# A LayerNorm, attention and mixture-of-experts block on one core: normalising on GpSimd, turning by DMA, and the output projection by half batches

## The reference

```python
xn = _layernorm(x)
q = (xn @ Wq + bq).reshape(B, T, 8, 128)
k, v = split(xn @ Wkv + bkv)
q, k = q + pe, k + pe
probs = softmax(causal(q @ k.T / sqrt(128)))
s = (probs @ v) @ Wo                      # heads side by side
logits = xn @ router_w + router_b         # the two largest of 8 are kept
y = sum_e gating[e] * (relu(xn @ w1[e] + b1[e]) @ w2[e] + b2[e])
x = x + s * silu(y)
```

## Time and profile before

| | us |
|---|---|
| median of 3 runs | 1088.56 (1087.25 to 1088.9) |
| the profiled execution | 1086.89 |
| its span, first to last instruction | 1085.0 |
| TensorE's granted clock, mean | 0.999 of full |

### The profile page before, as it was taken

One profiled execution on the slowest core, in us unless ns is written; L12 is line 12 of the kernel. 1 busy time (PEld: TensorE's weight loads), 2 busy tenths in 40 slices (PEclk: granted clock), 3 DMA queues, 4 the chain that ended last, 5 costly groups with the idle time before them and its releaser, 6 DMA issues.

```text
span 1085.0 us, 25159 instructions
## 1 busy us (share of the span) xinstructions
PE 995.2 (92%) x8734; PEld 783.7 (72%) x8734; DVE 859.1 (79%) x1543; ACT 644.6 (59%) x1360; POOL 324.9 (30%) x339
## 2 busy tenths in 40 slices
PE   1647999999999999998889889999999999999997
PEld 1536888888888898965656667767677677777776
DVE  6885777666766555569999999998999999999971
ACT  3812333233333333348888888878888888888860
POOL 0005999899994200020011102121112111112111
PEclk9999999999999999999999999999999999999999
DMA  8548776766665312137897888998999879898992
GB/s 281 178 192 182 154 186 172 173 175 178 178 171 157 89 50 55 37 102 147 165 162 141 158 159 177 164 149 153 171 185 178 148 147 170 160 173 160 175 183 90
DMA packets 402810, 168.80 MB, mean 156 GB/s; under 512 B 345562, under 2 KB 393252, under 8 KB 402052
## 3 DMA queue, kind: packets, MB, share of 16 engines
q1 hardware_dynamic: 345632, 127.04, 56.1%
q10 hardware_dynamic: 50580, 22.45, 8.6%
q0 software_dynamic: 6480, 17.70, 6.6%
HBM read 51.66 MB, written 30.67 MB: 76 GB/s over the span
## 4 chain that ended last, share of the span: by engine, by line
PE 35%; DVE 13%; DMA 3%; ACT 3%; issue 2%; SPq 0%; ACTq 0%; DVEq 0%
PE b_psS L1144 10%; PE b_psO L1167 10%; PE b_psJ L1183 5%; PE b_psJ L1101 4%; DVE b_ph L1383 4%; DVE b_nmax L1347 4%; DMA b_pT<-b_ph 3%; PE b_psS L1194 2%; PE b_psS L1101 1%; PE b_psO L1169 1%; DVE b_outs L1389 1%; ACT b_pr L1252 1%; ACT b_ph L1282 1%; DVE b_psJ L1356 1%; PE b_psS L1147 1%
## 5 line engine op out<-in xcount | busy, mean ns | idle before, releaser
L847 PE MATMUL psU<-bxT,w_p 128*128 128x256 f16 (+1 forms) x1920 | 287.9, 263 | 13.3 <-DVE w_p L273 10.4
L922 ACT ACTIVATE h<-psU,bias 128x256 f32<-128x256 f32 (+1 forms) x320 | 124.7, 447 | 284.9 <-PE psU L847 192.8
L856 PE MATMUL psY<-w_p,hp 128*128 x1704 | 272.4, 273 | 1.8 <-DVE hp L944 1.3
L1144 PE MATMUL b_psS<-b_kp,b_Q 128*128 128x512 f16 (+3 forms) x1152 | 218.4, 326 | 0.1
L847 PEld LDWEIGHTS psU<-bxT,w_p 128*128 x1920 | 189.1, 98 | 33.8 <-issue 15.1
L1252 ACT ACTIVATE b_pr<-b_psS,b_nmax 128x1024 f32<-128x1024 f32 (+7 forms) x256 | 186.7, 734 | 42.4 <-DVE b_nmax L1347 22.8
L1167 PE MATMUL b_psO<-b_pT,b_vp 128*128 128x256 f16 x1536 | 188.6, 272 | 18.1 <-issue 8.4
L1383 DVE SCALAR_TENSOR_TENSOR b_ph<-b_pr,b_rrec,b_ph 128x1024 f16<-128x1024 f32 (+7 forms) x256 | 199.1, 809 | 0.0
L1282 ACT ACTIVATE b_ph<-b_pr,b_rrec 128x1024 f16<-128x1024 f32 (+7 forms) x256 | 187.0, 768 | 15.9 <-DVE b_rrec L1376 15.6
L942 DVE CAST hp<-h 128x512 f16<-128x512 f32 (+1 forms) x160 | 88.5, 553 | 134.0 <-ACT h L922 127.1
L1347 DVE TENSOR_REDUCE b_nmax<-b_psS 128x1 f32<-128x1024 f32 (+7 forms) x256 | 182.7, 745 | 9.2 <-PE b_psS L1147 7.3
(11 more groups left out here) (181 smaller groups left out, 1029.4 us busy)
## 6 DMA issues: line engine op xcount, KB each, us to landing
wstage<-in_L_ffn_w SPq DMA_DIRECT2D x48, 256.0 KB
expert_rows<-rowx SPq DMA_DIRECT2D x67, 128.0 KB
expert_outputs<-y ACTq DMA_DIRECT2D x31, 256.0 KB
a_x_all<-in_L_attn_x SPq DMA_DIRECT2D x8, 512.0 KB, 9.8
a_w_raw<-in_L_ffn_w SPq DMA_DIRECT2D x4, 1024.0 KB, 6.5
xn_split<-a_xp SPq DMA_DIRECT2D x4, 1024.0 KB, 4.9
xn_turned<-a_xT SPq DMA_DIRECT2D x3, 1024.0 KB, 12.8
b_x_row<-in_L_attn_x SPq DMA_DIRECT2D x24, 128.0 KB, 2.6
```

The source lines that it names most:

```text
L847: mm = eng.matmul(psU[w % U][:, g % 2, 0:tiles * P].rearrange("p (t r) -> p t r", t=tiles), weight(n, a * W1 + c * H + g * P, P), bxT[n % ...
L856: mm = eng.matmul(psY[n % 2][:, t, :], hp[n % 2][:, a, g, t * P:(t + 1) * P], weight(n, 2 * W1 + (2 * g + b) * D, D), start=(g == 0 and k ...
L922: a = eng.activation(h32[w % 4][:, g, 0:rows], psU[w % U][:, g, 0:rows], ACT.Relu, bias=bias[:, ds(e * HT + 2 * q + g, 1)], scale=1.0 / WS)
L1144: mm = eng.matmul(dst, Q[n % 3][:, a, u * P:(u + 1) * P], kb[:, c, lo:lo + w], start=(kk == 0), stop=(kk == 2 and not last))
```

## The change

**Routing.** The first eight pairs are normalised by GpSimd instead of DVE, which goes on to the second half's statistics at once. The pairs 0, 2, 4, ... 12 are turned by DMAs that SP issues ahead of its four row stores, and no longer by PE and ACT; PE, ACT and DVE keep the other nine. ACT's order is written anew, so that the second root comes after six high halves.

**Attention.** The output projection goes by half batches: from n = 5 on, at i = 4, `o_pair` makes two tiles through four heads, again 24 matmuls, but into all of `psJ`. Where it is the first half of the batch's heads, ACT copies the bank out (`o_part`, 128x512); where the second, DVE adds the bank to that copy (`o_sum`, 128x512), and GpSimd multiplies by the gates and adds x (`weighted`, `added`, both 128x512). There are 28 of these calls instead of 24, so `rows_out` has only heads 28 to 31 left. The gates come from n = 4 on, one a head, and three a head in heads 30 and 31, in order of the tiles. The first half of the last batch is weighted and added to x ahead of the closing. DVE's second `o_low` of a head moves behind the maxima of step 0. There is one `outs`, x of the last batch has its own place and is loaded in head 8, and ACT waits for the last expert output to be stored ahead of head 0.

The diff, cut to its core:

```diff
-    OUT_DVE = (TWOS - 3, TWOS - 1)
+    BY_DMA = tuple(range(0, TWOS - 2, 2))
+    BY_PE = tuple(p for p in range(TWOS) if p not in BY_DMA)
...
-        for p in range(TWOS):
-            turn(p)
-            if p == 3:
+        eng.wait_ge(s_rl, 1)
+        for e in range(len(BY_PE)):
+            turn(e)
+            if e == 1:
                 eng.wait_ge(s_br, 80)
-            if p >= 2:
-                logits(p - 2)
+            if 1 <= e <= 7:
+                logits(BY_PE[e - 1])
+            if e >= 2 and e - 2 < len(BY_DMA) - 1:
+                logits(BY_DMA[e - 2])
+        logits(BY_DMA[-1])
...
+        behind = {7: 1, 8: 3, 9: 5, 11: 7, 13: 9, 15: 11}
+        root(0)
+        for p in range(6):
+            high(p)
+        root(1)
+        for p in range(6, TWOS):
+            high(p)
+            if p in behind:
+                out(behind[p])
+        out(TWOS - 3)
+        out(TWOS - 1)
...
-        for p in range(4):
-            normal(p)
-            after(p)
         for g in (5, 6, 7):
             stats(g)
-            normal(g - 1)
-            after(g - 1)
         variance(NT, slice(HALF, NT))
-        normal(7)
-        after(7)
+        eng.wait_ge(s_rh, 1)
+        eng.scalar_tensor_tensor(rw_p[:, 1], rw_s[:, :, :], WS, rw_p[:, 0], ALU.mult, ALU.subtract).then_inc(s_rl, 1)
+        for p in range(4):
+            low(p)
         rstd(2, slice(HALF, NT))
         for p in range(8, TWOS):
             normal(p)
-            after(p)
-        for p in range(TWOS, TWOS + 3):
-            after(p)
+            low(p - 4)
+        for p in range(TWOS - 4, TWOS):
+            low(p)
+        out(TWOS - 2)
...
+        eng.wait_ge(s_rs, 1)
+        for p in range(TWOS // 2):
+            for t in (2 * p, 2 * p + 1):
+                a = eng.tensor_scalar(x_all[:, t, :], x_all[:, t, :], mv[:, t, 0:1], rs[:, 0, t:t + 1], ALU.subtract, ALU.mult)
+            a.then_inc(s_xp, 1)
...
+        for d, p in enumerate(BY_DMA):
+            low_done(eng, p)
+            if d >= 4:
+                eng.wait_ge(s_dt[d % 4], 16 * (d // 4))
+            eng.dma_start_transpose(turned(p).rearrange("p t h n -> p (t h) n"),
+                                    xp[:, 2 * p:2 * p + 2].rearrange("p t h d -> p (t h d)")).then_inc(s_dt[d % 4], 16)
...
-    seq = list(range(TILES, NT)) + list(range(TILES))
-    turn_of = {c: s for s, c in enumerate(seq)}
+    PART, MORE = HEADS // 2, TILES // 2
+    gates = [(5 * n + 1, n - PART) for n in range(PART, NH - 2)]
+    gates += [(5 * n + x, NT - 6 + 3 * (n - NH + 2) + x) for n in (NH - 2, NH - 1) for x in range(3)]
+    gate_at = dict(gates)
...
+        outs = sb("outs", [P, 2, HEADS, T], F16)
+        fin = sb("x_last", [P, QT, D], F32)
...
-            def o_tile(c):
+            def o_pair(r):
+                m, p = r // 4, r % 4
+                eng.wait_ge(al_, 2 * PART * (m + 1))
+                if r:
+                    bank_free(eng, r - 1)
+                h0 = PART * (m % 2)
+                for x in range(2):
+                    t = 2 * p + x
+                    for h in range(h0, h0 + PART):
+                        for kk, (a, e) in enumerate(PASSES):
+                            mm = eng.matmul(psJ[:, x * D:(x + 1) * D], outs[:, a, h, t * P:(t + 1) * P], wo_p[:, e, h, :],
+                                            start=(x == 0 and h == h0 and kk == 0), stop=(x == 1 and h == h0 + PART - 1 and kk == 2))
...
-                        if i == 0 and n >= HEADS + 2:
-                            eng.wait_ge(ot_, n - HEADS - 1)
+                        if i == 0 and n >= PART + 2:
+                            bank_free(eng, n - PART - 2)
                         project(*jobs.order[q], job_bank[jobs.bank[q]]).then_inc(jm_, 1)
-                    if i == 4 and n > HEADS:
+                    if i == 4 and n > PART:
                         eng.wait_ge(jl_, jobs.issued(k + 1))
-                        o_tile(n - HEADS - 1)
+                        o_pair(n - PART - 1)
...
-            rows_out(0, 0, HEADS - 2)
-            o_tile(TILES - 1)
+            rows_out(0, PART, HEADS - 2)
+            o_pair(NH - PART - 1)
...
-            rows_out(3, 0, HEADS - 1)
+            rows_out(3, PART, HEADS - 1)
...
-            rows_out(2, 0, HEADS - 1)
+            rows_out(2, PART, HEADS - 1)
...
-            rows_out(1, 0, HEADS - 1)
+            rows_out(1, PART, HEADS - 1)
...
+            def o_part(g):
+                eng.wait_ge(om_, 4 * (2 * (g // 4)) + g % 4 + 1)
+                if g >= 4:
+                    eng.wait_ge(oa_, g - 3)
+                eng.activation(part[g % 4][:, :, :].rearrange("p t d -> p (t d)"), psJ[:, :], ACT.Copy, scale=0.5 / WS).then_inc(oe_, 1)
...
+            for i, o in enumerate(v["y_o"]):
+                eng.wait_ge(o, 16 * len(range(i, NBLK, 3)))
...
+                if i == 0 and n >= PART + 2 and not two_of(n - PART - 2)[0]:
+                    o_part(two_of(n - PART - 2)[1])
...
-                if k < LAST and n:
-                    if i == 1:
-                        weigh(seq[n - 1])
-                    if i == 3:
-                        tanh(seq[n - 1])
-            weigh(TILES - 1)
-            tanh(TILES - 1)
+                if k in gate_at:
+                    weigh(gate_at[k])
+                if k - 2 in gate_at:
+                    tanh(gate_at[k - 2])
+            o_part(two_of(NH - PART - 1)[1])
...
-                if 2 <= c < TILES:
-                    eng.wait_ge(oa_, c - 1)
+                if 8 <= c < TILES:
+                    eng.wait_ge(oa_, c // 2 - 3)
...
+            def o_sum(g):
+                whole = part[g % 4][:, :, :].rearrange("p t d -> p (t d)")
+                eng.wait_ge(oe_, g + 1)
+                eng.wait_ge(om_, 4 * (2 * (g // 4) + 1) + g % 4 + 1)
+                eng.scalar_tensor_tensor(whole, psJ[:, :], 0.5 / WS, whole, ALU.mult, ALU.add).then_inc(ot_, 1)
...
-                if i == 0 and n >= HEADS + 2:
-                    o_gated(n - HEADS - 2)
+                if i == 0 and n >= PART + 2 and two_of(n - PART - 2)[0]:
+                    o_sum(two_of(n - PART - 2)[1])
...
-                if 6 <= k <= LAST and (k - 1) % 5 in (2, 4):
-                    o_low((k - 1) // 5 - 1, (k - 1) % 5 // 4)
+                if 6 <= k <= LAST and i == 3:
+                    o_low(n - 1, 0)
                 if k < LAST:
                     maxima(k)
+                if 6 <= k <= LAST and i == 0:
+                    o_low(n - 2, 1)
-                if k < LAST and n:
-                    if i == 2:
-                        whole_f(seq[n - 1])
-                    if i == 4:
-                        gated(seq[n - 1])
+                if k - 1 in gate_at:
+                    whole_f(gate_at[k - 1])
+                if k - 3 in gate_at:
+                    gated(gate_at[k - 3])
...
             o_low(NH - 1, 0)
+            eng.wait_ge(fe_, 4)
             closing(0)
...
+            def weighted(g):
+                eng.wait_ge(G_, max(turn_of[2 * g], turn_of[2 * g + 1]) + 1)
+                eng.tensor_tensor(flat(part[g % 4][:, :, :]), flat(part[g % 4][:, :, :]), flat(G_of(g)), ALU.mult).then_inc(og_, 1)
+                eng.wait_ge(og_, g + 1)
+            def added(g):
+                eng.wait_ge(ot_, g + 1)
+                weighted(g)
+                eng.wait_ge(xq[g % 3], 16 * (g // 3 + 1))
+                eng.tensor_tensor(flat(xr[g % 3][:, :, :]), flat(part[g % 4][:, :, :]), flat(xr[g % 3][:, :, :]), ALU.add).then_inc(oa_, 1)
...
+                if i == 1 and n >= PART + 2:
+                    second, g = two_of(n - PART - 2)
+                    if second:
+                        added(g)
+                    elif g >= MORE:
+                        added_last(g)
+                if k + 3 in gate_at:
+                    fetch(gate_at[k + 3])
+            added_last(MORE + 3)
...
-            eng.wait_ge(sc_, LAST)
-            eng.dma_start(fin[:, :, :], xf[:, TILES:, :]).then_inc(xf_, 16)
+                if i == 1 and n == HEADS:
+                    eng.dma_start(fin[:, :, :], xf[:, TILES:, :]).then_inc(xf_, 16)
```

172 lines of the change are left out of this document (75 added, 97 removed).

## The result

The changed kernel takes 1093.57 us in the median of 8 runs (1090.57 to 1102.04), the kernel before 1087.9 us in 8 runs beside them (1085.9 to 1095.13). The ratio is 1.0063, with a 95% interval from 1.0044 to 1.0081: 0.6% slower, where I had forecast 1% faster. The profiled execution took 1092.46 us, 5.6 us above that of before.

What follows compares the result with a forecast made beforehand. Bounds: routing's chain up to the logits, DVE in the first heads, PE from head 5 on. -4.4 - 3.5 + 4.5 + 1.5 + 2.3 - 10.4 = -10.0 us gave 1076.9, 1078.6 as median; range 1070 to 1087 us.

Steps and rivals of the forecast that it cites:

- Routing, -4.4 forecast: Routing up to the logits: last low half 7.2 us earlier, 2.8 given back behind it; between -6.5 and 0.
- signs of being wrong: Last head: PE waits for turned probabilities; routing: GpSimd's normalising over 0.7 us; heads 10 to 29 growing longer.
- ScalarE's saved copies: Routing: seven copies at 1.00 us that ACT no longer makes, said to count for nothing more.
- Heads 1 to 4, -3.5 forecast: DVE-bound first heads lose gates and a wait: 1.06 us a head in three, 0.3 in head 4; -4 to -1.5.
- the wait: Heads 1 to 3: DVE's 0.33 us wait goes with `o_low` behind the maxima.
- Heads 5 to 10, +4.5 forecast: `o_pair` brings PE 24 more matmuls a head: +3.6 in heads 5 to 7, +0.9 in 8 to 10; +3 to +6.
- later heads, +1.5 forecast: Heads after 10: same PE work, small costs from `o_part` and GpSimd beside DVE's low halves; between 0 and 10 us.
- Rival (b): GpSimd and DVE hinder each other behind the twelve `o_sum`: 1.7 us a head, 20 us, 3.3 in routing; 1099 us, chance 0.07.
- the cover that I named for `o_part`: Later heads: 1.46 us of score matmuls and the maxima behind them hide `o_part`; any excess would be paid 16 times.
- Heads 30 and 31 and the end, -8.1 forecast: Extra gates and gathers cost heads 30 and 31 +2.3 us; fewer output-projection matmuls at the end give -10.4.
- the 10.4 us: Behind head 31's scores: 96 fewer output-projection matmuls at 0.109 us, 10.5 us; taken as -10.4, between -10.5 and -6.
- rival (c): The end is DMA-bound: extra gathers and gates push the last turnings by 4 us, PE waits; 1082.6 us, chance 0.1.

Runs made afterwards that it cites:

- negated_mean: Changed kernel with VectorE writing the mean negated and all normalising as add-multiply instead of subtract-multiply: ratio 0.9990 to the kernel before, 7.9 us below the changed kernel.
- no_dma_turning: Changed kernel with add-multiply normalising, GpSimd's addition of x held back and `o_part` earlier, but without the seven DMA turnings: ratio 0.9990 to the kernel before.
- normal_by_dve: Changed kernel with VectorE normalising the first 16 tiles again, the seven pairs still turned by DMA: ratio 1.0070 to the kernel before.

## Why the prediction was wrong, point by point

**Routing, -4.4 forecast, +3.3 measured at the first expert matmul.** The step that failed is the price of GpSimd's instruction, 0.45 us from the 637 ns of a multiply-multiply form on twice the columns, with bounds 0.3 and 0.64. It took 1.22. I scaled by columns and carried the price from one pair of operations to another. That GpSimd's normalising takes over 0.7 us was also one of the prediction's own signs of being wrong. With a form that costs 0.55, negated_mean gave -4.5 there. The rest of the sum was right in kind, and the agreement with -4.4 is partly luck: the last low half came 6.0 us earlier (40.64) instead of 7.2, the logits followed 4.8 us behind it instead of 5.2 and came 3.6 us earlier, and the last 0.9 us of the -4.5 arose behind them, where nothing was changed. The DMA turnings landed in time: SP needed 1.23 us for one, not 2.3, and it landed 2.7 us behind the start of its issue in the median. It was also wrong to count ScalarE's saved copies for nothing: with the copies back, in the order that no_dma_turning gives ScalarE, the gain is gone.

**Heads 1 to 4, -3.5 forecast, -1.3 measured.** VectorE lost its gates, but heads 2 and 3 fell by 0.56 us, not 1.06. The term that failed is the wait: in head 2 VectorE is busy for 0.67 us less (0.73 were forecast), but its wait of 0.33 did not go, it became one of 0.26 and one of 0.16, both for ScalarE. That ScalarE's chain with VectorE over exponentials and sums now sets part of the head is my reading, no run tests it. Head 1 fell by 0.35 us here; in the traces in which the clock did not fall it took 15.9 us, so that heads 1 to 4 gave 2.2 (normal_by_dve). Head 4 grew by 0.2, where 0.3 less was forecast.

**Heads 5 to 10, +4.5 forecast, +6.3 measured; later heads, +1.5 forecast, +5.4 measured.** Two terms were too small. Contention of GpSimd with the low halves: I took it as part of 1.5, and the trace shows 0.5 us in head 18 and 4.4 us in the twelve heads together, of which 0.3 were forecast as PE's work. Rival (b) had its mechanism and its place right and its price of 1.7 us a head three to five times too high. And the cover that I named for `o_part`, 1.46 us of score matmuls, was measured from the wrong end: ScalarE isn't free when `o_pair` ends, but 1.2 us later, since its order is fixed. Moving `o_part` gained 0.55 us in eight heads. That heads 10 to 29 grow was another of the signs of being wrong.

**Heads 30 and 31 and the end, -8.1 forecast, -6.2 measured.** From the first `rows_out` matmuls to the end it is 28.1 us instead of 36.6, so 8.5 of the 10.4 us came; the 1.82 us before `o_part` are what is missing. Behind head 31's scores the turned probabilities were in time, against rival (c). Within head 31 they were not, the third sign of being wrong: PE waits 2.53 us before the value products of head 30, where the longest wait of before was 1.02.

```profile
1050.47 2.45 PE L1200 MATMUL b_psO<-b_pT,b_vp 128*128 128x256 f16 x21 [2.53 <-issue]
```

Head 31 up to the first `rows_out` grew by 1.0 us by this and its gates, close to the 1.1 forecast.

**The forecast as a whole.** The three causes that I had priced wrong are worth 7.9, 2.1 and 6.6 us by the edits' ratios one by one. With all three removed the kernel ran in 1078.84 us. That it comes so near to the 1078.6 forecast is luck in part: its trace, of the slowest run, has heads 1 to 4 at -0.3 (the clock was low in head 1) and head 30 at +3.6 against before, and its six runs spread over 11 us. The range held none of this because each bound was drawn from the nearest row and not from what differed in it, and because the three fell on the same side.

## What to carry to other kernels

A price for an engine on which a form of instruction has not yet run is a guess however near the row seems: operation pair and operands have to be the same, and where they aren't, the range must take in a factor of two or three. When a bank or buffer is handed back by an in-order engine, the time that counts is when that engine gets to the instruction, not when its inputs are ready. And in this kernel two-input work on GpSimd did least harm beside VectorE instructions that read PSUM.
